# Listing the expert rows chunk by chunk, so that experts run beside the scans, with a row-wise combination under the last shared groups

## The chip, the cores and the metric

The kernel runs on one core of one Trainium2 chip. A core has a matrix engine (PE, whose weight loads stand apart as PEld), a vector engine (DVE), an activation engine (ACT), GpSimd (POOL) and a queue of transfers on SyncE (SP); each runs its own instructions in order and waits on semaphores. The metric is the device time of one execution in microseconds.

## The reference, cut to what matters

All arrays are float32. 4096 tokens of width 256 lie in four rows of 1024. A first layer (projection, convolution over three tokens, a scan over time with 16 states per channel, a gated projection) is added to x; then comes a mixture of experts, each token through its two best experts of eight, beside a shared feed-forward.

```python
        s = A_t * s + Bx_t                      # the scan: 16 states for each of 256 channels
    ...
        y = C * ssum + D_param * xs
        return jnp.einsum('btd,ed->bte', y, W_out) * jax.nn.silu(z)
...
        probs = jax.nn.softmax(logits.astype(jnp.float32), axis=-1)
        top_w, sel = jax.lax.top_k(probs, TOP_K)               # TOP_K = 2, 8 experts
        top_w = top_w / jnp.sum(top_w, axis=-1, keepdims=True)
...
        h = jax.nn.gelu(jnp.einsum('th,ehf->tef', x_flat, W1) + b1[None], approximate=False)
        y = jnp.einsum('tef,efh->teh', h, W2) + b2[None]       # 256 -> 1024 -> 256
        out = jnp.einsum('teh,te->th', y, combine)
        sh = jax.nn.gelu(x_flat @ sW1 + sb1, approximate=False)
        out = out + sh @ sW2 + sb2
...
    x = x + _layernorm(_L0_attn_ref(_layernorm(x, axis=-1), ...), axis=-1)
    x = x + _layernorm(_L0_ffn_ref(_layernorm(x, axis=-1), ...), axis=-1)
```

## The kernel before

`timetable()` writes one list of steps, PLAN, and each engine walks through it and emits its own part of every step. So PLAN's order is the order on every engine.

The tokens go in eight chunks of 512 (NC, TC). For chunk i, `prep(i)` normalises and projects, `main(i)` runs 32 scans of 512 tokens (16 states, two halves of the channels), and `post(i)` makes the layer's output, adds the residual, stores the normalised row in `xn_d`, and takes the router's logits. In `main`, PE spreads a state's row over the partitions (`spread`, L596), DVE multiplies (`mult`, L881) and scans (L900), ACT makes the decays (L1139), and POOL adds the states up (L1225). Between the scans of chunk i stand prep(i+1), post(i-1) and, one step to a scan, the shared feed-forward of chunks already posted: `s1` (L640) and `s2` (L655), in groups of 256 tokens. A Gelu needs another table on ACT than the decays do, so beside the scans a group's values are first copied with their bias and then passed through one Gelu between two table loads (`s_gelu`, L1167).

After the last scan come post(7), then the routing of all tokens at once: `top2`, `count`, and one-hot matrices OHp and OHq, whose 64 products (`table`, L668) put each expert's list of rows into columns. Then 39 tiles (NTILE) of 256 rows (ROWS), each with one expert: `gather` (L1242) brings the rows by index, `turn` (L683) transposes them, `up` (L696) and `down` (L708) multiply, `scatter` (L1250) writes the results by token to `z_d`; `weights` (L1322 to L1325) loads 2 MB of an expert's weights for each tile, two tiles ahead. Last, `load_z` reads `z_d` back and `combine` (L737) adds shared part and the two weighted experts on PE, by diagonal matrices; statistics (L811), normalisation (L1067) and the sum (L1042) follow.

PSUM has eight banks of 512 columns: three for the scans, five (NGEN) that PLAN's other steps take in turn, and take again when the instruction named by `emptied` is done.

## Time and profile before

| what | value |
|---|---|
| median of 3 runs | 1411.81 us (1407.17 to 2218.4) |
| the profiled execution | 1411.27 us |
| its span, first to last instruction | 1409.3 us |
| mean granted PE clock | 0.874 |
| PE, DVE, ACT, POOL busy | 82%, 53%, 42%, 38% |
| moved by DMA | 152.17 MB |

A busy share is a mean over stages that differ. Up to the last scan DVE is nearly always busy and PE at times; after it PE is, and DVE rests. A clock of 1.00 is 2.4 GHz for PE and 0.50 is 1.2 GHz; a mean between them is a mixture. Time outside the span is 1411.27 - 1409.3 = 2.0 us.

### The profile page before, as it was taken

To read this page: it belongs to the slowest core of one execution; us is meant where nothing else is said; L and a number is where in the kernel's file an instruction comes from. 1 tells how busy PE (TensorE), PEld (TensorE's weight loads), DVE (VectorE), ACT (ScalarE), POOL (GpSimd) and SP (SyncE) were. 2 spreads that over 40 slices of the span, in tenths; PEclk is the share of its full clock that TensorE was granted. 3 is DMA by queue.
4 is the path that set the end of the run, shared out by engine and by line. 5 is a ranking of instruction groups with operands and counts; after the bars stand their busy time and mean duration, and the time that the engine had idled before them with its cause. 6 is when DMAs were issued, how large, how long until landed. Compare 5 with 4: busy or idle time off the path is not lost.

```text
span 1409.3 us, 14491 instructions
## 1 busy us (share of the span) xinstructions
PE 1155.3 (82%) x4810; PEld 905.8 (64%) x4810; DVE 745.4 (53%) x1281; ACT 590.5 (42%) x1057; POOL 542.3 (38%) x589
## 2 busy tenths in 40 slices
PE   4444687786868679683968899999999999999996
PEld 2112265563636556362857788888888888888874
DVE  2899988889898999979448111111111111111016
ACT  2563675756757576664440022222222221212113
POOL 0465655646575565647200232322222232323111
PEclk9575778897988979796977699999999999999998
DMA  4000101001020100001012355586666664656446
GB/s 132 29 1 1 45 1 45 30 22 54 8 68 1 45 30 29 32 9 52 11 50 77 96 188 202 180 265 230 216 223 221 223 223 167 211 175 210 160 151 207
DMA packets 117834, 152.17 MB, mean 108 GB/s; under 512 B 15207, under 2 KB 102592, under 8 KB 117761
## 3 DMA queue, kind: packets, MB, share of 16 engines
q1 hardware_dynamic: 110272, 132.63, 29.1%
q0 software_dynamic: 7488, 18.63, 3.6%
q8 instruction: 38, 0.62, 0.2%
q14 instruction: 36, 0.29, 0.1%
HBM read 126.06 MB, written 27.00 MB: 109 GB/s over the span
## 4 chain that ended last, share of the span: by engine, by line
PE 60%; DVE 23%; issue 11%; ACT 3%; POOL 1%; DMA 1%; SPq 1%; DVEq 0%; POOLq 0%
PE psum L696 19%; PE psum L708 19%; DVE S L900 8%; PE psum L640 6%; DVE psum L881 5%; PE psum L655 3%; DVE stats L811 2%; PE psum L668 2%; PE psum L737 1%; PE psum L610 1%; PE psum L683 1%; PE psum L570 1%; PE psum L596 1%; ACT A L1139 1%; ACT hT L1167 1%
## 5 line engine op out<-in xcount | busy, mean ns | idle before, releaser
L1225 POOL TENSOR_TENSOR Ssum<-Ssum,S 128x512 f32<-128x512 f32 x240 | 302.9, 1268 | 114.5 <-DVE S L900 114.3
L1181 ACT ACTIVATE h<-psum,bb 128x256 f32<-128x256 f32 x312 | 130.7, 470 | 474.6 <-PE psum L696 474.6
L696 PE MATMUL psum<-XT,w 128*128 128x256 f32 x1248 | 277.7, 381 | 0.9 <-DVE XT L1014 0.9
L708 PE MATMUL psum<-w,h 128*128 128x256 f32 x1248 | 275.8, 379 | 0.0
L696 PEld LDWEIGHTS psum<-XT,w 128*128 128x128 f32 x1248 | 238.4, 191 | 34.0 <-DVE XT L1014 1.3
L708 PEld LDWEIGHTS psum<-w,h 128*128 128x128 f32 x1248 | 234.2, 190 | 30.3
L1250 POOL DMA_INDIRECT z_d<-y,ids x78 | 78.4, 1005 | 389.1 <-DVE y L1022 375.4
L596 PE MATMUL psum<-bst,SEL 96*128 96x512 bf16 x128 | 60.1, 478 | 187.9 <-DVE S L900 157.5
L1139 ACT ACTIVATE A<-dts,nea 128x512 f32<-128x512 f32 x256 | 173.1, 715 | 89.7 <-DVE S L900 80.1
L881 DVE TENSOR_TENSOR psum<-us,psum 128x512 f32<-128x512 f32 x256 | 162.9, 680 | 6.9 <-PE psum L596 5.6
L596 PEld LDWEIGHTS psum<-bst,SEL 96*128 96x128 bf16 x128 | 13.0, 102 | 230.7 <-DVE S L900 184.8
L1022 DVE TENSOR_TENSOR y<-bb,psum 128x256 f32<-128x256 f32 x78 | 29.3, 417 | 249.3 <-PE psum L708 249.3
L1014 DVE COPY XT<-psum 128x512 f32<-128x512 f32 x39 | 27.0, 691 | 245.7 <-PE psum L683 245.7
L900 DVE TENSOR_TENSOR_SCAN S<-A,carry,psum 128x512 f32<-128x512 f32 x120 | 149.0, 1264 | 0.0
L640 PE MATMUL psum<-nT,s 128*128 128x256 f32 x512 | 144.1, 444 | 0.5 <-DVE dts L869 0.5
L900 DVE TENSOR_TENSOR_SCAN S<-A,psum 128x512 f32<-128x512 f32 x120 | 141.7, 1203 | 0.0
L640 PEld LDWEIGHTS psum<-nT,s 128*128 128x128 f32 x512 | 115.3, 227 | 32.1 <-ACT hT L1160 8.3
L655 PE MATMUL psum<-s,hT 128*128 128x256 f32 x512 | 121.9, 390 | 0.0
L1242 POOL DMA_INDIRECT G<-xn_d,idg x78 | 76.9, 985 | 98.1 <-DVE q L1003 74.6
L655 PEld LDWEIGHTS psum<-s,hT 128*128 128x128 f32 x512 | 99.4, 196 | 23.2 <-issue 4.9
L1160 ACT ACTIVATE hT<-psum,sb1t 128x256 f32<-128x256 f32 x128 | 52.8, 470 | 57.7 <-PE psum L640 57.7
L1197 POOL TENSOR_TENSOR rs<-rs,C 128x4 f32<-128x4 f32 (+1 forms) x28 | 31.0, 1107 | 106.7 <-DVE rs L820 106.7
(151 smaller groups left out, 1129.3 us busy)
## 6 DMA issues: line engine op xcount, KB each, us to landing
w<-W SPq DMA_DIRECT2D x78, 1024.0 KB, 7.5
Z<-z_d SPq DMA_DIRECT2D x32, 256.0 KB, 7.0
bb<-b SPq DMA_DIRECT2D x39, 128.0 KB, 8.2
xnb<-x SPq DMA_DIRECT2D x16, 256.0 KB, 3.7
Xr<-x SPq DMA_DIRECT2D x16, 256.0 KB, 3.1
x_d<-gb SPq DMA_DIRECT2D x8, 512.0 KB, 2.9
xn_d<-nb SPq DMA_DIRECT2D x8, 512.0 KB, 3.2
sh_d<-O SPq DMA_DIRECT2D x16, 256.0 KB, 2.1
```

What stands on the lines that cost most here:

```text
L596: eng.matmul(BB[m % 2], SEL[:, n:n + 1].to_broadcast([96, 128]), bst[i % 2], start=True, stop=True).then_inc(spread, 1)
L640: t = eng.matmul(ps[:, 256 * ff:256 * ff + 256], s1[:, k, 128 * (f + ff):128 * (f + ff) + 128], nT[i % 3][:, k, 256 * q:256 * q + 256], st ...
L655: t = eng.matmul(bank(g)[:, 256 * j:256 * j + 256], hT[n % 2][:, f, 128 * j:128 * j + 128], s2[:, f, :], start=f == 0, stop=f == 7)
L696: i = eng.matmul(PS[3 + m % 3][:, 256 * ff:256 * ff + 256], w1[n % 2][:, k, 128 * (f + ff):128 * (f + ff) + 128], xT[n % 2][:, k, :], star ...
L708: i = eng.matmul(PS[6 + n % 2][:, 256 * j:256 * j + 256], h[n % 2][:, f, 128 * j:128 * j + 128], w2[n % 2][:, f, :], start=f == 0, stop=f ...
L881: eng.tensor_tensor(bb if c else UB, us[i % 2][:, c, :], bb, ALU.mult).then_inc(mult, 1)
L900: eng.tensor_tensor_scan(to, A[m % NA], BB[(m // 2) % 2] if c else UB, first, ALU.mult, ALU.add).then_inc(scan, 1)
L1139: eng.activation(A[m % NA], dts[i % 2][:, c, :], ACT.Exp, scale=nea[:, c, n:n + 1]).then_inc(decay, 1)
L1181: eng.activation(h[n % 2][:, f + ff, :], PS[3 + m % 3][:, 256 * ff:256 * ff + 256], ACT.Gelu, bias=bb1[n % 2][:, f + ff:f + ff + 1]).then_ ...
L1225: eng.tensor_tensor(to, to, of, ALU.add).then_inc(nsum, 1)
L1242: eng.indirect_dma_start(G[n % 3][:, j, :], None, xn_d, bass.IndirectOffsetOnAxis(ap=idg[:, 2 * n + j:2 * n + j + 1].bitcast(u32), axis=0) ...
L1250: eng.indirect_dma_start(z_d, bass.IndirectOffsetOnAxis(ap=ids[:, 2 * n + j:2 * n + j + 1].bitcast(u32), axis=0), y[n % 3][:, j, :], None, ...
```

## The change

A row's place in its expert's list is now known as soon as its chunk is routed. Each expert has a region in a list in memory, `list_d`, of 8-byte entries (token to read, row to write). `route(i)` follows post(i): the two best experts of 512 tokens, a running count `filled` that gives each row its place, and eight indirect writes of 128 entries (`table`). `select` then names, for this chunk, the next QUOTA[i] halves of 128 rows that are full whatever the data is: 0, 9, 8, 8, 8, 8, 8 of them for chunks 0 to 6, and the last 23 after chunk 7, when part-filled ones count too: 72 halves (NHALF) in place of 39 tiles. Unfilled entries keep the values that one transfer, `lists<-PADS`, writes at the start.

Two halves make a duo, whose halves may belong to two experts: `up` multiplies 128 columns at a time, and each half has its own w1 (three buffers) and w2 (two). A duo goes through the same steps as a group of 256 shared tokens, with bias copy and separate Gelu while scans run. The plan takes shared groups and duos in turn: duos 0 to 15 and the shared groups of chunks 0 to 5 stand beside the scans, duos 16 to 35 after them, and the shared groups of chunks 6 and 7 (LATE) at the very end. Beside the scans of chunks 3 to 7 three steps of this work stand to two scans, before one to one. A and S have five buffers in place of six; post(i-1) stands in scans 1 to 17, before in 2 to 27.

The combination leaves PE: DVE computes shared + w * z row by row (`mix`, four instructions for 256 tokens), for chunks 6 and 7 before their shared part (`premix`).

```diff
-ROWS = 256
-NTILE = (2 * T + E * (ROWS - 1)) // ROWS
-NCOL = NTILE * ROWS // 128
...
+QUOTA = [0] + [-(-(2 * TC * (i + 1) - E * 127) // 128) for i in range(1, NC)]
+QUOTA = [0] + [QUOTA[i] - QUOTA[i - 1] for i in range(1, NC)]
+
+NHALF = (2 * T + E * 127) // 128
+NHALF += NHALF % 2
+QUOTA[NC - 1] = NHALF - sum(QUOTA[:NC - 1])
+LISTED = [sum(QUOTA[:i + 1]) for i in range(NC)]
+NDUO = NHALF // 2
+LROWS = E * (T // 128) + 32
...
-NA, NS = 6, 6
-FIRST_POST, LAST_POST, LAST_PREP = 2, 27, 29
...
+NA, NS = 5, 5
+NG, NID, NW, NV = 4, 12, 3, 2
+FIRST_POST, LAST_POST, FIRST_PREP, LAST_PREP = 1, 17, 4, 29
+LATE = 6
+WAITING = 6
+NGEN, NALL = 5, 8
...
+        if i < LATE:
+            waiting_s.extend([("s", i, 0), ("s", i, 1)])
...
+    def route(i):
+        while i not in posted:
+            yield
+        say("top2", i)
+        say("soft", i)
+        yield
+        g = next(use)
+        say("count", i, g)
+        yield
+        say("weigh", i)
+        say("place", i, g)
+        yield
+        if QUOTA[i]:
+            say("select", i)
+        for n in range(8):
+            say("table", i, n)
+            yield
+        listed[0] = LISTED[i]
+        yield
...
+    def fetch():
+
+        while fetched["rows"] < min(listed[0], 2 * turned[0] + NG):
+            h = fetched["rows"]
+            say("ids", h)
+            later(2, "gather", h)
+            ready_at[h] = now[0] + WAITING
+            fetched["rows"] += 1
+        while fetched["w1"] < min(listed[0], 2 * upped[0] + NW):
+            h = fetched["w1"]
+            say("fetch1", h)
+            ready_at[h] = max(ready_at.get(h, 0), now[0] + WAITING)
+            fetched["w1"] += 1
+        while fetched["w2"] < min(listed[0], 2 * downed[0] + NV):
+            say("fetch2", fetched["w2"])
+            fetched["w2"] += 1
...
+    def pick():
+        fetch()
+        m = duos[0]
+        duo = (m < NDUO and fetched["rows"] >= 2 * m + 2 and fetched["w1"] >= 2 * m + 2
+               and now[0] >= ready_at[2 * m + 1])
+        after_duo = bool(groups) and groups[-1][0] == "d"
+        if waiting_s and (not duo or len(waiting_s) >= 4 or (after_duo and not direct[0])):
+            groups.append(waiting_s.pop(0))
+        elif duo:
+            duos[0] += 1
+            groups.append(("d", m))
+        elif m == NDUO and late_s:
+            groups.append(late_s.pop(0))
+        else:
+            return None
+        return len(groups) - 1
...
+    def down(n):
...
+            say("down", n, part, g)
+            yield
+        say("down_out", n, g)
+        if groups[n][0] == "d":
+            downed[0] += 1
+            later(1, "scatter", n)
+        elif groups[n][1] < LATE:
+            later(1, "store", n)
...
-                part(beside, 1)
+                part(beside, 1 if i < 3 else 1 + k % 2)
...
-        part(beside, 3)
...
+        tick()
+        part(beside, 2)
+    direct[0], room_for[0] = True, NALL
+    say("widen")
+    while listed[0] < NHALF:
+        next(routing)
+        tick()
+        part(beside, 1)
+    for n, _ in enumerate(beside):
+        tick()
+        if late_s and n % 8 == 4 and n // 8 < NC:
+            say("load_s", n // 8)
+        if downed[0] == NDUO:
+            break
+    while agenda:
+        tick()
+    say("load_z")
+    final = finishing(say)
+    part(final, NC - LATE)
+    for n, _ in enumerate(beside):
+        tick()
+
+        if 6 <= n < 6 + 2 * LATE:
+            part(final, 1)
+    for _ in final:
         pass
...
+def finishing(say):
+    for i in range(LATE, NC):
+        say("premix", i)
+        yield
+    order = list(range(NC))
+    for n, i in enumerate(order):
+        if i < LATE:
+            say("mix", i)
+        say("stats", 4, i)
+        yield
+        if n:
+            say("normal", 4, order[n - 1], False)
+        say("scales", 4, i)
+        if n:
+            say("result", order[n - 1])
+        yield
+    say("normal", 4, order[-1], True)
+    say("result", order[-1])
+
...
+    list_d = nc.dram_tensor("list_d", [LROWS * 128, 2], i32, kind="Internal").ap()
+    lists = list_d.rearrange("(r p) w -> p r w", p=128)
...
+                        m, = what
+                        h, f0 = 2 * m + u // 2, 4 * (u % 2)
+                        if u == 0:
+                            eng.wait_ge(turn_out, m + 1)
+                        if u % 2 == 0:
+                            eng.wait_ge(got_w1[h % NW], 32 * (h // NW + 1))
+                        for f in range(4):
+                            for k in range(2):
+                                t = eng.matmul(ps[:, 128 * f:128 * f + 128],
+                                               w1[h % NW][:, k, 128 * (f0 + f):128 * (f0 + f) + 128],
+                                               XT[m % 2][:, u // 2, k, :], start=k == 0, stop=k == 1)
+                    t.then_inc(full[BANK[g]], 1)
+                elif step == "down":
...
+                    if kind == "s" and what[0] >= LATE:
+                        i, q = what
+                        eng.wait_ge(premix, 4 * (i - LATE) + 2 * q + 2)
+                        to = Z[2 * i + q][0]
+                        eng.tensor_tensor(to.rearrange("p j d -> p (j d)"), to.rearrange("p j d -> p (j d)"), bank(g),
+                                          ALU.add).then_inc(down_out, 1)
...
+                elif step == "premix":
+                    i, = a
+                    eng.wait_ge(weigh, WEIGH * NC)
+                    for n in (2 * i, 2 * i + 1):
+                        eng.wait_ge(got_z[n], 32)
+                        for k in range(2):
+                            for j in range(2):
+                                t = eng.scalar_tensor_tensor(Z[n][0][:, j, :], Z[n][k][:, j, :],
+                                                             wts[:, k, 2 * n + j:2 * n + j + 1],
+                                                             Z[n][0][:, j, :] if k else sb2t, ALU.mult, ALU.add)
+                            t.then_inc(premix, 1)
+                            eng.wait_ge(premix, 4 * (i - LATE) + 2 * (n - 2 * i) + k + 1)
...
+                elif step == "mix":
+                    i, = a
+                    for n in (2 * i, 2 * i + 1):
+                        eng.wait_ge(got_z[n], 32)
+                        eng.wait_ge(got_l[i], 64)
+                        if n == 0:
+                            eng.wait_ge(weigh, WEIGH * NC)
+                        for k in range(2):
+                            for j in range(2):
+                                t = eng.scalar_tensor_tensor(SS[n][:, j, :] if k == 0 else Z[n][0][:, j, :],
+                                                             Z[n][k][:, j, :], wts[:, k, 2 * n + j:2 * n + j + 1],
+                                                             SS[n][:, j, :], ALU.mult, ALU.add)
+                            t.then_inc(mix, 1)
+                            eng.wait_ge(mix, 2 * n + k + 1)
...
+                elif step == "table":
+                    i, n = a
+                    if n == 0:
+                        eng.wait_ge(place, PLACE * (i + 1))
+                        if i == 0:
+                            eng.wait_ge(padded, 16)
+                            eng.wait_ge(got_val, 16)
+                    eng.indirect_dma_start(
+                        list_d, bass.IndirectOffsetOnAxis(ap=posi[:, 8 * i + n:8 * i + n + 1].bitcast(u32), axis=0),
+                        VAL[:, 32 * (n // 4) + 4 * i + n % 4, :], None).then_inc(tabled[i], 16)
...
+            eng.wait_ge(pads_set, 2)
+            eng.dma_start(lists, PADS).then_inc(padded, 16)
...
+                elif step == "ids":
+                    h, = a
+                    i = chunk_of(h)
+                    eng.wait_ge(select, SELECT * i)
+                    if h == LISTED[i] - QUOTA[i]:
+                        for j in range(i + 1) if i == 1 else (i,):
+                            eng.wait_ge(tabled[j], 128)
+                    if h >= NG:
+                        eng.wait_ge(got_g[h % NG], 16 * (h // NG))
+                    if h >= NID:
+                        wait_stored(eng, NTH["d", (h - NID) // 2])
+                    r = eng.value_load(trow[0:1, h:h + 1], min_val=0, max_val=LROWS - 1)
+                    eng.dma_start(ID[h % NID], lists[:, bass.ds(r, 1), :].squeeze(1)).then_inc(got_id[h % NG], 16)
+                elif step == "fetch1":
+                    h, = a
+                    if h >= NW:
+                        eng.wait_ge(up_out, 4 * NTH["d", (h - NW) // 2] + 2 * ((h - NW) % 2) + 2)
+                    eng.wait_ge(select, SELECT * chunk_of(h))
+                    e = eng.value_load(texp[0:1, h:h + 1], min_val=0, max_val=E - 1)
+                    eng.dma_start(w1[h % NW], w1v[bass.ds(e, 1)].squeeze(0)).then_inc(got_w1[h % NW], 16)
+                    eng.dma_start(bb1[h % NW], b1[bass.ds(e, 1)].squeeze(0)).then_inc(got_w1[h % NW], 16)
+                elif step == "fetch2":
+                    h, = a
+                    if h >= NV:
+                        eng.wait_ge(down_out, NTH["d", (h - NV) // 2] + 1)
+                    eng.wait_ge(select, SELECT * chunk_of(h))
+                    e = eng.value_load(texp[0:1, h:h + 1], min_val=0, max_val=E - 1)
+                    eng.dma_start(w2[h % NV], w2v[bass.ds(e, 1)].squeeze(0)).then_inc(got_w2[h % NV], 16)
+                    eng.dma_start(bb2[h % NV], b2[bass.ds(e, 1)].to_broadcast([128, D])).then_inc(got_w2[h % NV], 16)
```

SP, the start of the program, before: the constants C, cw, wxz and wx, for which the engines wait, stand behind x and hx.

```order
L1261 DMA xnb<-x 128x2x256 x2
L1265 DMA hx<-x 2x256 x4
L1266 DMA C<-cst 128x650
L1267 DMA cw<-conv_w 128x2x3
L1268 DMA wxz<-W_inT 128x2x512
```

SP, the same place now: PADS is written out as 128x288 entries of two 4-byte numbers.

```order
L1394 DMA xnb<-x 128x2x256 x2
L1398 DMA list_d<-PADS 128x288x2
L1400 DMA hx<-x 2x256 x4
L1401 DMA C<-cst 128x441
L1402 DMA cw<-conv_w 128x2x3
L1403 DMA wxz<-W_inT 128x2x512
```

The initial write stands ahead of hx and of every constant, on the same queue.

PE, beside the scans of chunk 4, before: `spread` is the row with SEL, s_60 and s_61 are the shared weights.

```order
L596 MATMUL psum<-bst_118,SEL 128x512
L601 MATMUL psum<-dcb_117,wdc 128x512
L640 MATMUL psum<-nT_96,s_60 128x256 x4
L601 MATMUL psum<-dcb_117,wdc 128x512
L655 MATMUL psum<-s_61,hT_98 128x256 x4
L596 MATMUL psum<-bst_118,SEL 128x512
L655 MATMUL psum<-s_61,hT_98 128x256 x8
L596 MATMUL psum<-bst_118,SEL 128x512
```

PE, the same place now: w_149 and w_150 are w1 of two halves, w_152 and w_153 their w2.

```order
L841 MATMUL psum<-w_153,hT_134 128x256 x8
L740 MATMUL psum<-bst_169,SEL 128x512 x2
L794 MATMUL psum<-C,G_140 128x128 x2
L794 MATMUL psum<-C,G_141 128x128 x2
L745 MATMUL psum<-dcb_168,wdc 128x512 x2
L819 MATMUL psum<-XT_143,w_149 128x128 x16
L740 MATMUL psum<-bst_169,SEL 128x512
L819 MATMUL psum<-XT_143,w_150 128x128 x8
L754 MATMUL psum<-wout,yb 128x256 x4
L819 MATMUL psum<-XT_143,w_150 128x128 x8
L841 MATMUL psum<-s_62,hT_133 128x256 x4
L740 MATMUL psum<-bst_169,SEL 128x512
```

A duo's transposes and multiplications have come between the spreads, so that more of PE's work lies between one spread and the next.

SP, in the stretch of experts, before: what one tile of 256 rows fetches.

```order
L1321 TENSOR_LOAD texp
L1321 ISA x2
L1322 ISA
L1322 DMA w_177<-W 128x2x1024
L1323 DMA w_179<-W 128x8x256
L1324 ISA
L1324 DMA bb_181<-b 128x8
L1325 ISA
L1325 DMA bb_183<-b 128x256
```

SP, the same place now: what one half of 128 rows fetches, w1 and w2 each with its own reading of the expert's number (a duo has each of these pieces twice).

```order
L1469 TENSOR_LOAD texp
L1469 ISA x2
L1470 ISA
L1470 DMA w_151<-W 128x2x1024
L1471 ISA
L1471 DMA bb_146<-b 128x8
...
L1477 TENSOR_LOAD texp
L1477 ISA x2
L1478 ISA
L1478 DMA w_152<-W 128x8x256
L1479 ISA
L1479 DMA bb_147<-b 128x256
```

256 rows now bring 4 MB of weights where they brought 2 MB, and w2 of a duo waits for the preceding duo's `down_out`.

## Rows read from the trace of the kernel before

**Rows 1.** The page: busy time of each engine, and the chain that ended last.

```profile
PE 1155.3 (82%) x4810; PEld 905.8 (64%) x4810; DVE 745.4 (53%) x1281; ACT 590.5 (42%) x1057; POOL 542.3 (38%) x589
...
PE 60%; DVE 23%; issue 11%; ACT 3%; POOL 1%; DMA 1%; SPq 1%; DVEq 0%; POOLq 0%
```

**Rows 2.** By stage: stretch, length, PE, PEld, DVE, ACT, POOL busy, clock, DMA share, GB/s.

```profile
47.40:112.50 65.10, 27.28 (x60) 11.01 (x60) 64.78 (x87) 37.50 (x59) 44.01 (x65) 0.63 0.05 16
112.50:194.80 82.30, 50.79 (x160) 30.94 (x160) 75.20 (x113) 45.81 (x75) 46.64 (x38) 0.71 0.06 20
194.80:278.50 83.70, 65.67 (x232) 44.75 (x232) 74.98 (x116) 56.03 (x91) 49.91 (x69) 0.80 0.10 32
...
444.10:526.50 82.40, 63.24 (x232) 42.89 (x232) 76.47 (x116) 56.03 (x91) 45.61 (x37) 0.83 0.10 32
...
608.00:678.70 70.70, 45.66 (x168) 33.40 (x169) 65.24 (x92) 36.38 (x62) 40.66 (x33) 0.73 0.09 30
...
721.00:794.50 73.50, 60.24 (x265) 55.08 (x265) 40.56 (x72) 12.62 (x22) 5.02 (x5) 0.71 0.23 76
794.50:1352.00 557.50, 557.48 (x2648) 490.35 (x2648) 67.42 (x178) 130.72 (x312) 148.22 (x149) 1.00 0.59 196
1352.00:1409.30 57.30, 42.20 (x161) 30.15 (x160) 27.97 (x94) 13.19 (x28) 8.54 (x6) 0.91 0.68 220
```

**Rows 3.** Waits of 50 to 670 us: who waited for whom, us, times, longest.

```profile
PE psum L596 <- DVE S L900: 157.5, 56, 7.0
...
DVE psum L881 <- PE psum L596: 5.6, 10, 1.4
```

**Rows 4.** PE in order of time, one expert tile: start, length, instruction, count.

```profile
953.28 7.07 PE L696 MATMUL psum<-XT,w 128*128 128x256 f32 x32
960.19 0.60 PE L683 MATMUL psum<-C,G 128*128 128x128 f32 x4
960.62 7.07 PE L708 MATMUL psum<-w,h 128*128 128x256 f32 x32
967.53 7.07 PE L696 MATMUL psum<-XT,w 128*128 128x256 f32 x32
```

**Rows 5.** DMA queues of 1200 to 1270 us: packets, MB, share of 16 engines.

```profile
q1 hardware_dynamic: 7918, 10.83, 47.5%
q0 software_dynamic: 960, 2.38, 8.7%
```

**Rows 6.** DMA packets of 7.4 to 8.4 us, and of 4.4 to 8.9 us.

```profile
DMA packets 1252, 0.18 MB, mean 176 GB/s; under 512 B 1219, under 2 KB 1222, under 8 KB 1252
...
DMA packets 2113, 1.02 MB, mean 226 GB/s; under 512 B 1680, under 2 KB 1746, under 8 KB 2113
```

**Rows 7.** Groups of instructions by form: count, busy us, mean ns, idle before.

```profile
L1014 DVE COPY XT<-psum 128x512 f32<-128x512 f32 x39 | 27.0, 691 | 245.7 <-PE psum L683 245.7
L1022 DVE TENSOR_TENSOR y<-bb,psum 128x256 f32<-128x256 f32 x78 | 29.3, 417 | 249.3 <-PE psum L708 249.3
...
L756 DVE SCALAR_TENSOR_TENSOR nm<-mv,rs 128x4 f32<-128x4 f32 x24 | 5.6, 235 | 2.9 <-POOL rs L1197 2.9
...
L1181 ACT ACTIVATE h<-psum,bb 128x256 f32<-128x256 f32 x312 | 130.7, 470 | 474.6 <-PE psum L696 474.6
L1167 ACT ACTIVATE hT<-hT 128x2048 f32<-128x2048 f32 x15 | 28.7, 1911 | 0.2
L1167 ACT ACT_TABLE_LOAD x15 | 19.2, 1283 | 0.3
...
L1150 ACT COPY lg<-psum 128x32 f32<-128x32 f32 x8 | 1.5, 185 | 5.9 <-PE psum L630 5.3
...
L1242 POOL DMA_INDIRECT G<-xn_d,idg x78 | 76.9, 985 | 98.1 <-DVE q L1003 74.6
```

**Rows 8.** Everything in order of time, 1352 us to the end.

```profile
1352.11 0.75 DVE L1022 TENSOR_TENSOR y<-bb,psum 128x256 f32<-128x256 f32 x2 [13.06 <-PE psum L708]
...
1360.56 1.99 PE L737 MATMUL psum<-Z,DG 128*128 128x256 f32 x8 [0.34 <-DMA Z<-z_d]
...
1371.90 1.42 DVE L811 BATCH_NORM_STATS2 stats<-psum 128x6 f32<-128x256 f32 x4
...
1378.76 2.49 DVE L1042 TENSOR_TENSOR XX<-XX,SS 128x512 f32<-128x512 f32 x4
```

More of the change, by code:

```diff
@@ L191, in timetable @@
     use = itertools.count()
-    beside = shared()
+    beside = feed_forward()
+    routing = (step for i in range(NC) for step in route(i))
     for _ in prep(0):
@@ L287, in emptied @@
         return "lg_out", i + 1
-    if step == "s1":
-        return "s1_out", 8 * (2 * i + n) + a[2] + 2
-    if step == "s2" and a[2] == 3:
-        return "s2_out", 2 * (2 * i + n) + 2
+    if step == "count":
+        return "place", PLACE * (i + 1)
+    if step == "turn":
+        return "turn_out", i + 1
+    if step == "up":
+        return "up_out", 4 * i + n + 1
+    if step == "down" and n == 3:
+        return "down_out", i + 1
 def banks():
-    where, turns, before, held, last, at = {}, {}, {}, set(), {}, -1
+    where, turns, before, held, last, at, size = {}, {}, {}, set(), {}, -1, NGEN
@@ L309, in banks @@
         elif step in GIVING:
             held.discard(where[used(step, a)])
[L311 to L314 removed]
+    return where, turns, before
+PLAN, GROUPS = timetable()
 EMPTIED = {row[-1]: e for row in PLAN if (e := emptied(row[0], row[1:]))}
[L316 to L324 removed]
```

914 lines of the change are left out of this document (420 added, 494 removed).

## The prediction

> **What bounds the kernel now.** I read the busy shares first, then the windows by stage, the waits, one expert tile in order of time, and the DMA queues. PE carries 60% of the chain that ended last and DVE 23% [rows 1], so two stages with two bounds stand one behind the other. Up to the last scan at 678.7 us DVE is the bound: in a chunk of 82.4 us it is busy 76.5, PE 63.2 at a clock of 0.83, ACT 56.0, POOL 45.6 [rows 2]. There `spread` waits 157.5 us for the scans, and the multiplications only 5.6 for `spread` [rows 3]. Each chunk so leaves PE 30 us at full clock: 82.4 - 63.2 x 0.83 = 29.9. From 794.5 us on PE is the bound, 557.48 of 557.5 us at clock 1.00, while DVE does 67 [rows 2]. Between them lie post(7) and the routing, 678.7 to 794.5, and behind them the combination, 57.3 us. The change fills the first stage with work of the second, so I ask what a chunk costs once PE is full, what is left behind the scans, and what each end costs.
>
> **A duo against a tile.** Before, a tile takes 967.53 - 953.28 = 14.25 us: 32 instructions of `up` in 6.91, four transposes in 0.43, 32 of `down` in 6.91 [rows 4]. A fp32 product is two instructions. A duo has the same `down`; `up` has 64 instructions of 128 columns for 32 of 256. Whether that costs anything hangs on the weight load, as long for 128 columns as for 256. The transposes show it: a load of 128x128 and 128 columns streamed, four in 0.43 us, 0.107 each, half of 0.216 [rows 4]. 64 x 0.107 = 6.9 us: nothing is added, a duo is 14.3 us of PE. 36 duos for 39 tiles save 3 x 14.25 = 43 us of PE, and the 64 one-hot products and PE's combination go too.
>
> The Trainium skill, "TensorE: Matmul & The Clock Gate", section "The mechanism", says that a weight load overlaps matmuls in flight only where the row groups differ; here they never do. By that rule each 128-column instruction would cost load and stream in turn. The transposes speak against it, the first rival below prices it.
>
> **The start.** `lists<-PADS` is 128 x 288 = 36,864 pieces of 8 bytes on SP's queue, ahead of every constant that the engines wait for. No row shows 8-byte writes to memory. The densest stretch of small packets is 1252 in 1.0 us, all 16 DMA engines busy; a looser one has 2113 in 4.5 [rows 6]. That gives 36,864 / 1252 = 29 us, or at 470 per us 78. I take 35, near the first, since that one was limited by the engines and the other by how fast SP issued. First scan: 47.4 + 35 = 82 us.
>
> The Trainium skill, "DMA: Bandwidth & Descriptors", section "Specifications", adds that below 512 B the engine reads, changes and writes; a write of 8 bytes could by that be dearer than my 35 us, which is part of rival 3. No row here has one.
>
> **The scans.** Chunk 0 stays 65.1 us. Each routing adds to DVE some 41 dependent instructions of about 0.2 us (0.235 for a 4-column one, [rows 7]) = 8.4 us, fewer in chunks 1 and 2, which have no `select` or a shorter row: 82.3 + 6 = 88 and 83.7 + 8 = 92. In chunks 3 to 6 come three duos each as well:
> PE 63.2 x 0.83 + 3 x 14.3 = 95.4 at full clock.
> DVE 76.5 + 8.4 + 3 x (0.69 + 2 x 0.417) = 89.5 [rows 2, 7], and the 6 us that it idles now: 95.
> ACT 56.0 + 3 x (16 copies of about 0.31, between 0.185 for 32 columns and 0.470 for 256, + Gelu 1.9 + two table loads 2.6) = 84 [rows 7].
> POOL 45.6 + 20 indirect transfers of 1.0 (8 lists, 6 gathers, 6 scatters) = 66.
> Three engines of 95, 95 and 84 us stand in order and wait for each other: PE's `up` for ACT to empty a bank, `spread` behind 1.7 to 3.5 us of duo work, DVE's `turn_out` and `down_out` for PE. The floor is 97. To size the loss I laid the same durations on both orders, four scans at a time, and added up the busiest engine of each piece: 81.4 for a chunk before (82.4 measured), 104 to 108 for a chunk now. Two scans at a time gives 92 before, too much, and 119 to 127 now; that is the ceiling. I take 108. Chunk 7 has no prep: 70.7 + 22 = 93. Sum 65 + 88 + 92 + 4 x 108 + 93 = 770 us, before 678.7 - 47.4 = 631: the scans pay 139 us. One A and one S buffer less (five for six) are inside that loss; they would cost first where ACT's Gelu holds the decays for 4.5 us against 4 scans of cover.
>
> **After the scans.** post(7) keeps its 42 us: its chain of waits was 42 before and two duos fill PE. The routing of the last chunk lies beside duos 18 to 23, which are listed already, so the old routing stretch (73.5 us) goes. In it PE also did shared work, which is now either earlier or last. Left up to the last `down`: 18 duos and five pieces of `up`: 18 x 14.3 + 5 x 1.7 = 265 us of PE. Here the weights double. In 1200 to 1270 five tiles take 47.5% of 70 us on the hardware queue and 8.7% on the software one: 6.65 + 1.22 us of all 16 engines a tile [rows 5]. A duo has 2 x 6.65 + 1.2 = 14.5, and the loads for the end (28 x 256 KB, 1 us a duo) make 15.5, over PE's 14.3. Since w2 may only be fetched after the preceding `down_out`, gaps come in: I take 15.7, ends 14.3 (hidden) and 18.5 (3 us of gap). 265 + 18 x 1.4 = 290.
>
> **The end.** Before, from the last tile's y at 1352.1 to the first combination is 8.5 us, and the rest is 49 [rows 8]. Now DVE does it all: 64 mixing instructions of 128x256 at 0.41 (as `down_out`'s, [rows 7]) = 26; statistics 32 x 0.36 + 8 x 0.8 = 18; 16 sums x 0.62 = 10; four `down_out` 2.7 [rows 8]. 57 us, where PE has 48 of shared work beside it: 8.5 + 57 + 2.5 for the last store + some waits = 70 us. The combination isn't hidden; it is the longer of the two.
>
> **Sum.** 82 + 770 + 42 + 290 + 70 = 1254 us of span, plus 2.0 around it: 1256 us, against 1411.3 of the profiled execution, which is 0.5 below the median: -11%. The scans get 139 us longer and the start 35; what follows the scans falls from 730.6 to 402.
>
> **The rivals.**
> 1. Slower: the load isn't hidden under 128 columns. Each of 36 x 64 = 2304 instructions costs 0.107 us more: +247, 1503 us. It decides from 0.067 us more on, 0.174 per instruction, where the gain is gone. For it: the load's own row is as long as 0.19 us, and no fp32 product of 128 columns is in the trace. Against it: the four transposes in 0.43 [rows 4].
> 2. Coupling: the in-order queues cost the ceiling, 122 us a chunk and 105 for chunk 7: +68, 1324. For it: three engines within 12% of each other. Against: PE has double-buffered `spread` and five banks.
> 3. Transfers: 18.5 us a duo behind the scans and 78 for the lists: +50 and +43, 1349 with both, about 1305 with one.
> 4. Faster: PE's surplus hides all, 98 us a chunk, 14.3 a duo: -40 and -25, 1190.
> 5. The change doesn't do what it says: duos wait for lists and weights beside the scans, and stand there as idle time; the scans grow while PE still has the work behind. With half of the 16 duos' time lost, 8 x 14.3 = +114: 1370.
>
> **Chances.** Forecast as worked (1205 to 1290) 0.56; rival 2 0.14; rival 3 0.10; rival 4 0.10; rival 5 0.05; rival 1 0.05. The range 1180 to 1345 holds the first four but for edges, about 0.82. A measurement of this kernel tells about 2% (1384 to 1440) from no change. Faster by over 2%: 0.91; within: 0.04; slower: 0.05, rival 1.
>
> **What would show it.** First scan at 70 to 90 us. Windows of chunks 3 to 6: 104 to 112 us, PE over 90% busy at a clock near 1.00, DVE near 85%. 64 instructions of `up` in 6.9 us where PE is full. Behind the scans PE busy over 88%, DMA share over 0.9, duos 15 to 16.5 us apart. DVE as the last engine of the chain for the final 60 us. The prediction falls if `up` has instructions 0.2 us apart at full clock, if the first scan comes after 125 us, or if chunks with duos exceed 120 us.

## The result and the profile after

The changed kernel takes 1544.4 us (median of 4, 1539.0 to 1546.3) against 1410.5 for the kernel before: ratio 1.095, 95% interval 1.091 to 1.099. It is slower, where 1256 us was forecast. The profiled execution took 1539.0 us, its span 1537.1.

The windows by stage of the changed kernel, cut at the first scan, at each chunk's first scan, at the last scan, at the twentieth duo and at the last one; columns as in [rows 2].

```profile
0.00:104.40 104.40, 20.29 (x56) 11.14 (x56) 13.79 (x32) 18.73 (x32) 5.52 (x12) 0.97 1.12 47
104.40:169.60 65.20, 27.54 (x61) 11.17 (x62) 64.88 (x88) 37.04 (x58) 44.16 (x65) 0.63 0.06 17
169.60:268.70 99.10, 68.26 (x240) 47.23 (x239) 82.56 (x140) 56.52 (x91) 54.98 (x46) 0.76 0.06 19
268.70:368.20 99.50, 65.28 (x243) 44.56 (x242) 86.29 (x159) 56.63 (x91) 57.73 (x77) 0.81 0.08 24
...
634.80:771.80 137.00, 106.54 (x544) 86.75 (x544) 91.76 (x168) 82.48 (x148) 65.71 (x57) 0.89 0.42 129
...
1031.50:1161.90 130.40, 88.03 (x490) 78.02 (x490) 25.54 (x88) 37.77 (x86) 30.27 (x31) 0.86 0.62 183
1161.90:1452.90 291.00, 251.42 (x1633) 228.97 (x1634) 21.64 (x48) 76.35 (x264) 59.78 (x60) 0.98 0.85 285
1452.90:1537.10 84.20, 49.26 (x221) 42.51 (x219) 57.77 (x166) 24.97 (x54) 10.04 (x10) 0.82 0.46 150
```

Against the terms of the sum: the first scan comes at 104.4 us (forecast 82); the scans take 1031.5 - 104.4 = 927.1 us (770); what follows takes 505.6 (42 + 290 + 70 = 402). Together 22 + 157 + 104 = 283 us more than the span forecast. Chunks 3 to 6 take 137.2, 129.4, 137.0 and 136.7 us, over the 120 at which the prediction was said to fall. In none of them is an engine full: in chunk 5 DVE works 91.8 of 137.0 us, PE 106.5, ACT 82.5. So the work was sized well and the idle time was not.

The waits up to the last scan, of after. They answer to [rows 3]: before, `spread` waited 157.5 us for the scans and the scans' side 5.6 for `spread`.

```profile
PE psum L740 <- DVE S L1009: 80.0, 24, 7.6
DVE psum L990 <- PE psum L740: 71.2, 21, 10.4
...
DVE stats L920 <- POOL gb L1356: 49.7, 14, 10.6
```

PE and DVE now stand for each other by turns. The third row was 1.9 us in two waits before: statistics wait for GpSimd's residual sum `gb`. One such place in order of time, in chunk 5; first DVE, then GpSimd, then SP, then PE, each from its own timeline.

```profile
661.55 2.44 DVE L1009 TENSOR_TENSOR_SCAN S<-A,carry,psum 128x512 f32<-128x512 f32 x2
674.58 0.75 DVE L920 BATCH_NORM_STATS2 stats<-gb 128x6 f32<-128x256 f32 x2 [10.59 <-POOL gb L1356]
...
677.14 0.69 DVE L1105 COPY XT<-psum 128x512 f32<-128x512 f32 x1
```

```profile
673.28 2.48 POOL L1356 TENSOR_TENSOR gb<-Xr,gb 128x512 f32<-128x512 f32 x2 [5.31 <-DMA Xr<-x]
```

```profile
661.16 0.38 SPq L1478 DMA_DIRECT2D w<-W  x1
661.72 0.44 SPq L1479 DMA_DIRECT2D bb<-b  x1
662.99 0.37 SPq L1478 DMA_DIRECT2D w<-W  x1
663.54 1.11 SPq L1479 DMA_DIRECT2D bb<-b  x1
664.70 1.77 SPq L1434 DMA_DIRECT2D Xr<-x  x2
```

```profile
660.14 0.60 PE L682 MATMUL psum<-C,xnb 128*128 128x128 f32 x4
677.93 5.31 PE L819 MATMUL psum<-XT,w 128*128 128x128 f32 x32 [17.18 <-issue]
```

Read from below: PE stands 17.18 us because `up` needs XT, whose copy by DVE came at 677.14. DVE stood 10.59 us for `gb`; GpSimd stood for Xr; and SP issued Xr only at 664.70, behind two fetches of w2 that had waited for the preceding `down_out`. Xr then landed 8.6 us after its issue (median; 3.1 before), with the 2 MB of these fetches ahead of it. ScalarE stood 17.9 us for `up`. One load placed behind a waiting fetch in SP's queue so holds PE, DVE, GpSimd and ScalarE. Chunks 5, 6 and 7 and post(7) each show PE idle for 16.8 to 17.6 us in this way.

PE behind the scans, in order of time, to be held against [rows 4].

```profile
1257.02 7.38 PE L819 MATMUL psum<-XT,w 128*128 128x128 f32 x64 [1.06 <-DVE y L1126]
1265.68 7.14 PE L841 MATMUL psum<-w,hT 128*128 128x256 f32 x32 [1.28 <-ACT hT L1296]
1272.66 0.60 PE L794 MATMUL psum<-C,G 128*128 128x128 f32 x4
1274.32 7.38 PE L819 MATMUL psum<-XT,w 128*128 128x128 f32 x64 [1.06 <-DVE y L1126]
```

64 instructions of `up` take 7.38 us from the start of the first to the end of the last: one of 128 columns costs half of one of 256, and rival 1 is out. A duo takes 17.3 us, of which 2.34 are two waits: `turn`, `up` and `down` of a duo stand one behind the other, with nothing of another duo between them.

### The profile page after: what moved, and what is told of

Its sections match the earlier page's. It is cut to its first block and busy times, and to the rows that moved or that the text cites. A ratio compares the mean times of both kernels' runs of the same rounds, so it can differ in the third digit from the quotient of the medians.

```text
span 1537.1 us, 18244 instructions
## 1 busy us (share of the span) xinstructions
PE 1082.6 (70%) x5546; PEld 885.7 (58%) x5546; DVE 798.4 (52%) x1518; ACT 692.6 (45%) x1375; POOL 598.6 (39%) x647
## 5 line engine op out<-in xcount | busy, mean ns | idle before, releaser
L819 PE MATMUL psum<-XT,w 128*128 128x128 f32 x2304 | 293.1, 290 | 121.1 <-issue 99.0
L819 PEld LDWEIGHTS psum<-XT,w 128*128 128x128 f32 x2304 | 286.3, 206 | 140.6 <-issue 113.9
L841 PE MATMUL psum<-w,hT 128*128 128x256 f32 x1152 | 285.1, 407 | 78.9 <-issue 52.7
L1296 ACT ACTIVATE hT<-psum,bb 128x128 f32<-128x128 f32 x576 | 164.0, 371 | 390.6 <-PE psum L819 390.3
L841 PEld LDWEIGHTS psum<-w,hT 128*128 128x128 f32 x1152 | 233.2, 205 | 122.6 <-issue 64.4
L1374 POOL DMA_INDIRECT G<-xn_d,ID x72 | 71.0, 986 | 177.8 <-DMA ID<-list_d 163.7
L841 PE MATMUL psum<-s,hT 128*128 128x256 f32 x512 | 120.1, 388 | 22.0 <-ACT hT L1289 17.4
L1383 POOL DMA_INDIRECT z_d<-y,ID x72 | 72.5, 1007 | 148.1 <-DVE y L1126 123.1
L841 PEld LDWEIGHTS psum<-s,hT 128*128 128x128 f32 x512 | 98.6, 194 | 42.6 <-ACT hT L1289 17.8
L807 PE MATMUL psum<-nT,s 128*128 128x256 f32 x512 | 121.7, 393 | 0.7 <-DVE dts L978 0.7
L1320 POOL TENSOR_TENSOR rs<-rs,C 128x4 f32<-128x4 f32 x32 | 32.9, 1028 | 122.5 <-DVE rs L929 122.4
L1365 POOL DMA_INDIRECT list_d<-VAL,posi x64 | 63.8, 996 | 17.3 <-issue 8.7
```

Of the source, the lines that this page charges most:

```text
L807: t = eng.matmul(ps[:, 256 * f:256 * f + 256], s1[:, k, 128 * (2 * u + f):128 * (2 * u + f) + 128], nT[i % 3][:, k, 256 * q:256 * q + 256] ...
L819: t = eng.matmul(ps[:, 128 * f:128 * f + 128], w1[h % NW][:, k, 128 * (f0 + f):128 * (f0 + f) + 128], XT[m % 2][:, u // 2, k, :], start=k ...
L841: t = eng.matmul(bank(g)[:, 256 * k:256 * k + 256], hT[n % 2][:, f, 128 * k:128 * k + 128], w[:, f, :], start=f == 0, stop=f == 7)
L1296: t = eng.activation(hT[n % 2][:, f0 + f, 128 * k:128 * k + 128], ps[:, 128 * f:128 * f + 128], fn, bias=bb1[h % NW][:, f0 + f:f0 + f + 1])
L1365: eng.indirect_dma_start(list_d, bass.IndirectOffsetOnAxis(ap=posi[:, 8 * i + n:8 * i + n + 1].bitcast(u32), axis=0), VAL[:, 32 * (n // 4) ...
L1374: eng.indirect_dma_start(G[h % NG], None, xn_d[0:TC * (chunk_of(h) + 1), :], bass.IndirectOffsetOnAxis(ap=ID[h % NID][:, 0:1].bitcast(u32) ...
```

## The experiments

All variants of the changed kernel from the second on hold the edit of the first. A chunk's time is from its first scan to the next chunk's.

**1. Contiguous lists.**

```diff
-eng.dma_start(lists, PADS)
+eng.dma_start(list_d.rearrange("(p r) w -> p r w", p=128), PADS)
```

> The changed kernel, but the 36,864 pairs that fill the lists are written in one contiguous run per partition (128 runs of 2304 B) instead of 8 bytes at a time; every pair has the same value, so the lists are the same. Theory: in the profile of the changed kernel the next transfer on SP's queue was held for 54.6 us behind that write and the first scan came at 104.4 us, so the first scan now comes at 50 to 54 us and the time falls by about 50, to 1494. Rival: the start was late for another reason (the constants' own transfers); then less than 10 us come back.

1487.1 us, 57.3 less. The first scan comes at 45.8, 58.6 us earlier, and every chunk keeps its length to 0.1 us (chunk 5 again 137.0). Behind the last scan the profiled execution takes 511.4 us where it took 505.6. The 8-byte pieces cost 58.6 us at the start.

**2. Xr ahead of the weights.** SP issues `Xr<-x` at `cmat(i, 0)` instead of at `residual`.

> As the run with contiguous lists, and besides SP issues the residual's loads Xr<-x at the first instruction of post, ahead of the weight fetches whose waits hold SP, instead of at the residual. Theory (SP's queue carries the coupling): the stop of 17 us that chunks 5, 6 and 7 and post(7) each show in PE goes, chunks 5 to 7 fall from 130-137 to 115-122 us, and the time falls by 50 to 65 against contiguous lists alone, to about 1435. Rival (the three in-order engines with 84 to 95 us of work each are what costs, as rival 2 of the prediction had it): the idle time comes back elsewhere, chunks stay above 128, time above 1480.

1457.8 us, 29 less. The chain is real: DVE's wait for `gb` in chunk 5 falls from 11.2 to 5.7 us, and the stops of 17 us in PE shrink (the longest there is 11.8). But chunks 4 to 7 are 129.4, 132.4, 133.1 and 117.5 where they were 129.4, 137.0, 136.7 and 123.0: 4 to 6 us in each of the three chunks that had the stop, not 13 to 17. Most of the removed stop comes back at other waits (DVE for `spread` 18.7 us where it was 17.4, PE's idle 26 of 132). Neither side's time held, though chunks 5 and 6 stay above 128 us as the rival has it: in the scans the queue's place costs 14 us (927.2 to 913.5) of the 157 that they take too long, behind them 11.

**3. Tail in another order.** The plan drops its six steps between a fetch and its use behind the scans.

```diff
-ready_at[h] = max(ready_at.get(h, 0), now[0] + WAITING)
+ready_at[h] = max(ready_at.get(h, 0), now[0] + (0 if direct[0] else WAITING))
```

> As the run with contiguous lists, but once the last scan is over the plan no longer asks for six steps between a weight fetch and its use. The order on PE behind the scans is then up(n+1) ahead of down(n) instead of turn, up, down of one duo in series. Theory (the order costs): the two idle times of 1.06 and 1.28 us per duo go and the period falls from 17.3 to between 15.0 and 16.3 us; 16.3 if the transfers are the bound (0.94 of 17.3 us), so 14 to 35 us less than contiguous lists alone, 1459 to 1480. Rival (transfers already set the period): it stays at 17.3, time 1494.

1487.0 us, no change, as the rival has it. The two waits of the serial order go and others take their place, as experiment 6 shows.

**4. No duo beside the scans.** `fetch` and `pick` leave duos out until the last scan is over.

> As the run with contiguous lists, but no duo and no fetch of rows or weights before the last scan; routing and lists stay beside the scans. It prices the routing alone and what a duo costs beside scans. Theory: chunks 3 to 7 take about 98 us as chunks 1 and 2 do now, so each of three duos cost 12 us beside the scans against 17.3 behind them, and 16 duos moved behind make the whole 60 to 90 us longer, 1555 to 1585. Rival: duos beside scans gain nothing, time 1494 within 15 us; or chunks stay above 110 without duos, then the routing is what made the scans long.

1569.4 us, as expected. Chunks 3 to 6 take 101.2 to 102.5 us. So three duos cost a chunk 137.0 - 102.0 = 35 us with Xr late and 30.4 with Xr early, about 10 each, against 17.3 behind the scans. Duos beside the scans do pay, 82 us for the 15 that end there. And the chunks without them are still 18 to 20 us longer than before.

**5. Light weights** (with 1 to 3): once each buffer has been filled, a fetch brings 32 of w1's 1024 columns and one of w2's eight slices. This kernel leaves out most of the weights; all instructions and waits stay. **6. The same with full weights.**

```diff
-eng.dma_start(w1[h % NW], w1v[bass.ds(e, 1)].squeeze(0))
+f1 = F if h < NW else 32
+eng.dma_start(w1[h % NW][:, :, 0:f1], w1v[bass.ds(e, 1)].squeeze(0)[:, :, 0:f1])
...
```

> Contiguous lists, Xr early and the tail order of the run before it, and besides a weight fetch moves 1/32 of w1 and 1/8 of w2 once each buffer has been filled once, so most duos compute with wrong weights; every instruction, wait and queue place stays. It takes the transfers alone out. Theory: the transfers and their buffers set the period of a duo behind the scans, the engines' order sets that of a chunk beside them. So duos behind the scans fall from 17.8 to 15.0 us (PE's 14.9), chunks 4 to 6 stay at 125 to 130 us: 1405 to 1420 us. Rival: the transfers are also what PE waits for beside the scans; then the chunks fall under 115 us too and the whole to 1350 or less.

> Contiguous lists, Xr early and the tail order together, full weights: the control for the run with light weights. Theory (transfers bound behind the scans): as contiguous lists with Xr early, 1453 to 1462 us, duos about 17.8 us apart. Rival: the tail order gains its 14 us now that SP is freer, 1440 to 1446.

1403.8 and 1462.9 us. Up to the last scan the two agree to 0.2 us in each chunk (132.5, 133.1, 117.5 for chunks 5 to 7): with Xr issued early, the weights' bytes cost nothing there. Behind the scans the duos are 14.5 us apart with light weights and 16.5 to 21.7 with full ones. The windows of 13 and of 14 duos, light and then full, each from its own run:

```profile
1100.90:1289.30 188.40, 188.40 (x1303) 177.66 (x1302) 18.79 (x40) 59.31 (x208) 47.87 (x49) 1.00 0.39 101
```

```profile
1107.10:1356.00 248.90, 214.17 (x1394) 193.58 (x1393) 19.48 (x41) 64.05 (x224) 51.77 (x52) 0.98 0.86 291
```

With light weights PE is busy all of the time. With full ones a duo takes 17.8 us, of which the DMA engines are busy 0.86, 15.3 us, and PE waits at each half's `down`:

```profile
1189.52 3.69 PE L841 MATMUL psum<-w,hT 128*128 128x256 f32 x16 [1.10 <-DMA bb<-b]
1193.81 3.72 PE L841 MATMUL psum<-w,hT 128*128 128x256 f32 x16 [0.60 <-DMA bb<-b]
```

**7. Neither duos nor routing beside the scans** (`part(routing, 1)` is gone from the scans).

> Contiguous lists, no duos and no routing beside the scans: all eight routings and lists stand behind the last scan. It prices what five S and A buffers for six and the moved post and prep cost alone. Theory: nothing; chunks 1 to 6 take 82 to 85 us as in the kernel before, so the routing cost 16 us a chunk in the run without duos beside the scans. Rival: the buffers or the moved steps cost; then chunks take 88 to 95 us and the routing alone costs 5 to 10. The whole comes out near 1560 (seven times 16 us less, eight routings in series more).

1633.4 us. My number for the whole was too low: the first duo ends only 108 us after the last scan. The chunks show the rival's effect, larger than it said: 95.7 us in chunks 1 and 2 and 98.8 to 99.6 in 3 to 6. The routing costs only 3 us a chunk (101.9 against 99.1 in the mean of chunks 3 to 6), so 12 to 17 us come from something that the prediction did not price at all.

**8. The softmax's Exp two steps later** (6 with a `yield` twice between `top2` and `soft`).

> Contiguous lists, Xr early and the tail order, and besides the softmax's Exp stands two steps later in the plan than the top-2 it waits for. Theory (routing's price is queueing, not work): ACT stood 3.8 us in a chunk waiting for VectorE's top-2 and VectorE then 4.5 to 5 us for ACT's bst; both go, each of chunks 1 to 7 gets 3 to 5 us shorter, 1425 to 1435 us against 1457. Rival: the time reappears at another wait, 1450 to 1460.

1429.6 us, 33 less than the control. In chunk 5 ScalarE's wait for the top-2 (3.6 us) is gone, DVE's for `spread` falls from 18.7 to 6.3 us, and the chunk from 132.5 to 123.2. The expected 3 to 5 us in each chunk did not come: chunks 1 and 2 grow from 99.1 and 99.5 to 102.9 and 102.6. Two things blur the run: the groups fall in another order (14 duos beside the scans, not 15), and the end of the scans falls inside a group, so that four of `up`'s instructions on ScalarE are copies whose Gelu this kernel leaves out. Experiments 12 and 13 differ by the same step with every Gelu in place, and there it gives 24 us.

**9 to 11. The kernel before with one part of the change.** Five A and S buffers (`NA, NS = 5, 5`); then the placement (post over steps 1 to 17, prep over 4 to 29); then both.

> The kernel before, with five A and five S buffers instead of six and nothing else. The run without routing beside the scans still had chunks of 96 to 99.6 us against 82.4 before, so something that the prediction put at nothing costs 14 to 17 us a chunk. Theory F: it is the buffers; then chunks take 94 to 99 us here and the whole is 1490 to 1525. Theory P (the denser placement of post and prep costs): chunks stay at 82 to 84 us, 1411 to 1420.

> The kernel before, six buffers, but post is placed over steps 1 to 17 of a chunk and prep over steps 4 to 29, as the change does, instead of 2 to 27 and 0 to 29. Theory P: chunks take 94 to 99 us, 1490 to 1525 in all. Theory F: chunks stay within 2 us of 82.4, 1400 to 1425. Both may share it, 88 us each.

> The kernel before, with five A and five S buffers and the dense placement of post and prep together. Theory I (they act together: ScalarE stands at a decay for a free A buffer while the copy that prep needs next is queued behind it): chunks take 96 to 99 us, 1490 to 1510 in all. Theory N (independent): 89 to 91 us a chunk as with the dense placement alone, 1448 to 1456.

1413.7 us (ratio 1.002, 1.001 to 1.003), 1450.6 (1.028, 1.025 to 1.031) and 1454.1 us (1.031, 1.028 to 1.034). Buffers alone (chunk 5), placement alone and both (chunk 4), with the same work and another length:

```profile
445.10:527.90 82.80, 62.05 (x232) 41.49 (x232) 76.61 (x117) 55.97 (x91) 45.63 (x37) 0.86 0.10 32
```

```profile
380.20:469.60 89.40, 61.16 (x233) 42.51 (x233) 75.19 (x116) 55.48 (x91) 49.81 (x69) 0.81 0.09 30
```

```profile
383.20:475.10 91.90, 63.59 (x233) 43.68 (x232) 75.29 (x116) 55.72 (x91) 49.78 (x69) 0.80 0.09 29
```

Buffers alone cost nothing, the dense placement 6 to 9 us a chunk (half of what Theory P had), and five buffers on top of it 0.5 to 3 more, as Theory N of the last run has it. In the dense chunk DVE has one wait that the same chunk of the kernel before lacks, for a copy by ScalarE. That it is what the placement costs is not shown:

```profile
DVE psum L860 <- ACT bst L1114: 5.4, 1, 5.4
```

**12. The changed kernel placed as before** (6, with `FIRST_POST, LAST_POST, FIRST_PREP, LAST_PREP = 2, 27, 0, 29`).

> The changed kernel with contiguous lists, Xr early and the tail order, and post and prep placed as in the kernel before (steps 2 to 27 and 0 to 29). Theory P: chunks 1 and 2 fall from 98 to about 85 us, those with duos from 130 to 115, 1360 to 1390 in all. Theory F: chunks stay as they are or get longer since routing comes later, 1450 to 1475.

1447.7 us, 15 less. Theory P was right in its sign and wrong in its size: chunk 1 falls from 99.1 to 93.5 us, chunk 2 stays at 99, chunks 3 to 6 fall from 129-137 to 123-127, and post(7) with what follows grows by 38 (498.5 to 536.8). Of that, post being later and 14 duos rather than 15 done are the part that the plan explains.

**13 to 15. Three rates of feed-forward steps** (12 with a later Exp in chunks 0 to 6; a group begun beside the scans keeps its separate Gelu to its end): one and a half steps per scan, one, two.

> Contiguous lists, Xr early, the tail order, post and prep placed as in the kernel before, and the softmax's Exp two steps behind its top-2 in chunks 0 to 6. Theory: wide placement and a later Exp each took stalls away (15 and 33 us); part of it is the same stall, so 1415 to 1430 us. Rival: they remove the same idle time, 1440 to 1450.

> As the run with wide placement and later Exp, with one step of the feed-forward per scan in all chunks instead of one and a half: 12 duos stand beside the scans instead of 16, two a chunk instead of three. Theory (a fixed price per duo): chunks fall by 10 us for the duo less, 4 duos more stand behind at 17.4, so 25 to 35 us slower than the run with one and a half steps. Rival (the price grows as the engines fill): chunks fall by 17 us or more and the whole stays the same or gets faster.

> As the run with wide placement and later Exp, with two steps of the feed-forward per scan from chunk 3 on. Groups run earlier; the lists still give four duos a chunk at most, 19 duos beside the scans instead of 16. Theory (fixed price): 3 duos less behind at 17.4, each paid with 10 beside: 15 to 25 us faster. Rival (price grows): the fourth duo of a chunk costs 17 us or more, same time or slower.

1423.9, 1426.1 and 1490.3 us. Here chunk 2, which has the routing but no duo, is at 91.7 us in all three. Chunk 5 at one, one and a half and two steps:

```profile
509.80:616.20 106.40, 93.85 (x434) 73.41 (x434) 91.78 (x164) 72.34 (x127) 59.79 (x51) 0.87 0.33 95
```

```profile
540.80:664.20 123.40, 108.06 (x545) 88.28 (x544) 93.88 (x167) 82.89 (x149) 65.80 (x57) 0.92 0.48 144
```

```profile
580.20:721.60 141.40, 121.08 (x607) 98.99 (x606) 92.28 (x169) 90.61 (x157) 67.85 (x59) 0.93 0.47 144
```

DVE's work is the same 92 to 94 us. With chunk 2 as the base, two duos cost 106.4 - 91.7 = 15 us, 7 each. The third costs 17, as much as behind the scans, which fits that 1423.9 and 1426.1 agree. The next 18 us buy 62 instructions more, six tenths of a duo, and are a clear loss. A fixed price per duo is refuted: the price grows. That it grows because the engines fill is the likely reading and not the only one, since the rate of steps rises with the duos, and experiment 18 shows that the rate alone can cost; no run separates the two. In the chunk of two steps DVE waits 33.0 us for `down` alone:

```profile
DVE y L1129 <- PE psum L844: 33.0, 5, 14.1
```

**16, 17. Fetches by halves.** Behind the scans w1 and w2 of a half are fetched again as soon as that half's products are done (a semaphore from TensorE after `down`'s second part; `bb2` is loaded with the odd half), at one and at one and a half steps.

> As the run with one step per scan (two duos a chunk, 24 to 25 behind the scans), but behind the scans w1 and w2 of a duo's first half are fetched again as soon as that half's products are done, not when the whole duo is. Same bytes. Theory (the moment of the fetch): duos behind the scans fall from 17.7 to 15.0 to 16.0 us, 24 of them give 40 to 65 us, 1360 to 1386 us, below the kernel before. Rival (the volume): period stays above 17, 1415 to 1430 us.

> As the run before it, with one and a half steps per scan (three duos a chunk, 19 to 20 behind). Theory: the third duo of a chunk costs 17 us beside the scans and now 15.5 behind them, so this is 0 to 12 us slower than with two, 1375 to 1395 us. Rival (the volume): 1415 to 1430 us.

1439.7 us, 14 slower than its control, and 1435.5 (median of four, 1432.2 to 1438.6; a fifth took 1454.6), 12 slower; at one step duos behind the scans are 15.8 to 22.9 us apart. Neither theory came true, but the runs do not test them: the edit moves w2 of the first half ahead and puts its `bb2` behind the second half's fetch, and TensorE waits for w2 and `bb2` together. One duo of experiment 16, SP and then PE:

```profile
1095.93 0.44 SPq L1498 DMA_DIRECT2D bb<-b  x1
1097.14 0.35 SPq L1500 DMA_DIRECT2D bb<-b  x1
...
1104.31 8.83 PE L854 MATMUL psum<-w,hT 128*128 128x256 f32 x32 [3.22 <-DMA bb<-b]
```

`down` starts 7.2 us after the last `bb2` is issued, and not when w2 is there. So what an earlier start of the bytes would gain stays open. In experiment 6 the order in time is this, again SP and then PE:

```profile
1199.06 0.38 SPq L1478 DMA_DIRECT2D w<-W  x1
...
1216.61 0.38 SPq L1478 DMA_DIRECT2D w<-W  x1
```

```profile
1206.33 3.69 PE L841 MATMUL psum<-w,hT 128*128 128x256 f32 x16 [1.22 <-DMA bb<-b]
1211.36 3.72 PE L841 MATMUL psum<-w,hT 128*128 128x256 f32 x16 [1.34 <-DMA bb<-b]
```

From a duo's first fetch of w2 to its `down` pass 7.3 us, to the end of `down` 8.8 more, and to the next duo's first fetch, which waits for this `down_out`, 1.5: a round of 17.55 us, the period that is seen. It is read from the trace and not tested.

No version of the changed kernel that does the whole work is faster than the kernel before; the nearest is 13, ratio 1.009 (1.006 to 1.012).

**18. Neither duos nor routing, placed as before.**

> As the run with no duos and no routing beside the scans (98.7 to 99.6 us a chunk), with post and prep placed as in the kernel before. Theory (all of the 16 us is placement): chunks 1 to 6 take 82 to 85 us and the whole falls from 1633 by about 100, to 1525 to 1545. Rival (placement is the 8 to 10 us it was in the kernel before, the rest is how the new plan cuts the shared work): 88 to 92 us a chunk, 1570 to 1590.

1583.0 us, the rival's time. Chunks 1 and 2 take 86.0 and 83.7 us: the placement gives back 10 of 13.5 us in the first and all of it in the second. Chunks 3 to 6 take 93.4 to 95.5. The one thing in the plan that changes at chunk 3 is the rate, one and a half feed-forward steps per scan for one. With no duo to place, the shared groups' steps come bunched: in chunks 3 to 6 the last four scans hold 83 to 86 of PE's shared instructions and take 18.5 to 19.7 us, in chunk 2 51 of them and 12.5 us. So the rate costs about 10 us a chunk here; no run holds it at one with the rest unchanged.

## Why the prediction was wrong

The step that failed is the price of the scans: 770 us forecast, 927.1 measured, 157 of the 283 us by which the span is too long. Two parts of it failed, a placement that stood in no term, and the figure for how long engines stand for each other.

**"Chunk 0 stays, each routing adds 6 to 8 us": the step left out the placement.** The diff moves post from steps 2 to 27 to steps 1 to 17 and prep's start from 0 to 4; my working has no term for it, and priced only added instructions. Chunk 0 did stay (65.2 us), and a routing cost 3 us, less than I took; chunks 1 and 2 came out at 99.1 and 99.5 for 88 and 92. The chunk of 137.0 us builds up so from 82.4: placement, five buffers and the new cut of the shared work +13.3 (95.7, chunks 1 and 2 of experiment 7), the rate with nothing to place +3.4 (99.1), routing +2.9 (102.0, experiment 4), three duos +30.4 (132.4, experiment 2), Xr behind the fetches +4.6. The differences depend on the order in which they are taken: with the wide placement the rate's share is 10, not 3.4.

**"I take 108, ceiling 122": the method failed, not the durations.** PE's 95.4 us at full clock, ACT's 84, DVE's 89.5 and POOL's 66 came out as 106.5 x 0.89 = 95, 82.5, 91.8 and 65.7 busy. I laid them on the order in windows of four scans and took the busiest engine of each, which presumes that engines inside a window never stand for each other. Two scans at a time, which I called the ceiling, gave 119 to 127, nearer but not a ceiling either. Rival 2 named the right kind of loss, with a chance of 0.14 and 68 us where the scans alone took 157 too long, part of which was the placement. With the wide placement, the later Exp and two duos, chunks 4 to 6 took 101 to 106 us: the spare 30 us of PE do carry two duos there. At the rate that a third needs they took 123.

**A queue was missing from the list of engines.** I priced SP's transfers by their bytes, and only behind the scans, and not by their places: SP waits in order like any engine, and Xr stood behind those waits. Experiment 5 shows that with Xr issued early the bytes cost nothing beside the scans; with Xr behind the fetches they were part of the stop, since it landed 8.6 us after its issue. The whole is small: 14 us in the scans, 11 behind them. I had named queues that a step is moved past only for the start.

**The start: mis-sized.** `lists<-PADS` cost 58.6 us where I took 35 between 29 and 78; both ends were right, the choice near the dense row was not. The run has 36,864 / 58.6 = 629 pieces per us, against 1252 in [rows 6]. The Trainium skill, "DMA: Bandwidth & Descriptors", section "Specifications", has it that a transfer below 512 B is read, changed and written. That does not tell the two rates apart, since 1219 of the 1252 packets of [rows 6] are below 512 B as well; no run here shows what makes the 8-byte writes slower.

**The duo behind the scans: 17.3 us for 15.7, inside 14.3 to 18.5.** PE's 14.3 was right: 14.5 with light weights. The DMA's 14.5 to 15.5 was right too: 15.3 (experiment 6), against [rows 5]. What I had not read from the order is that the plan runs a duo's three parts in series. Removing that left the duos at the same 17 to 18 us, held by the transfers (experiment 5). Two bounds lay on top of each other. The Trainium skill, "TensorE: Matmul & The Clock Gate", section "The mechanism", has it that a weight load overlaps products in flight only where the row groups differ. By that rule each 128-column product would pay for its load as well. This is not borne out: in experiment 6, 64 took 7.31 us with the clock at 1.00.

**"post(7) keeps its 42 us."** From the last scan to the twentieth duo pass 130.4 us for five duos, where my terms leave 42 + 290 - 16 x 15.7 = 81: the first ones are 31.1 and 41.2 us apart, and with light weights still 31.1, 27.9 and 36.0, so it is not the bytes. Post(7)'s chain and its order are left, with one Xr stop in it; no run takes them apart. The rest of the 104 us: 16 duos at 18.2 us for 15.7 (+40) and the end, 84.2 us for 70 (+14), though DVE worked 57.8 us there, for 57.

**Range and chances.** The time lies 199 us above the range. The slower side held one rival of 0.05, the weight load, which was wrong; the coupling that decided was on the list at a price that still left a gain. Rivals 2 and 3 together would have given 1324 + 93 = 1417, and I had added neither up nor asked what a chunk would cost if coupling went past the figure called a ceiling.

**What stays open.** Whether the round from w2's fetch to `down_out` is what keeps duos with full weights 17 to 18 us apart while the DMA engines are busy 0.86 of the time: experiments 16 and 17 left that round in place. What of the growing price of a duo is the rate and what the filling of the engines. And why the placement costs more in the new plan: experiment 18 gives 10 to 12 us back in chunks 1 and 2 by placement alone, where in the kernel before it cost 6 to 7, and the buffers under it 0.5 to 2.

## What to carry over

Idle time of the second engine is for sale only up to a point: here the first two duos of a chunk cost 7 us each, the third, with the rate that places it, 17, and the next more than it saved. When a plan's constants move existing steps closer together, price that first, even if no instruction is added: it cost more per chunk than the whole routing. List the queue that issues transfers among the in-order engines, and look at what stands behind each of its waits.

## What the runs showed of the hardware

The 36,864 writes of 8 bytes put the first scan back by 58.6 us, 629 pieces per us, with all 16 DMA engines busy meanwhile (a share of 1.12 of the first 104.4 us). SP's next `dma_start`s were held, for 55.43 us, and so everything behind them in the queue:

```profile
2.27 55.43 SPq L1400 DMA_DIRECT2D hx<-x  x4
57.74 4.97 SPq L1401 DMA_DIRECT2D C<-cst  x1
```

fp32 products of 128 columns run at 0.114 us each at full clock with a fresh 128x128 load for each (64 in 7.31 us), half of the 256-column ones (32 in 7.07). And 1 MB weight transfers beside the scans did not move a chunk by more than 0.2 us: chunk 5 took 132.5 us at a DMA share of 0.44 (experiment 6) and of 0.18 (experiment 5). Xr was issued early in both.
